# Per-example matrices made inside the loop, and the output put in order by ScalarE and VectorE, in a four-layer conditional residual kernel

## What is computed

```python
x = x + _L0_cond_ref(x, cond_128, ...)             # mixing
x = x + _L1_cond_ref(x, cond_128, ..., fside_S_0)  # convolution
x = x + _L2_cond_ref(x, cond_128, ...)             # mixing, other weights
x = x + _L3_cond_ref(x, cond_128, ..., fside_S_0)  # convolution, other weights

# mixing (L0, L2), K = 8
h = gelu(embedding @ W0 + b0); h = gelu(h @ W1 + b1)
att = softmax(h @ W2 + b2)
agg_w = einsum('bk,koi->boi', att, weight[..., 0]);  agg_b = att @ bias_k
out = einsum('boi,bih->boh', agg_w, x) + agg_b[:, :, None]

# convolution (L1, L3), 9 taps, 4 groups of 32 channels
out = conv(x, weight, padding=4, feature_group_count=4)
out = out + einsum('nd,od->no', c, c_weight)[:, :, None] + bias[None, :, None]
```

## Time and profile before

| | us |
|---|---|
| median of 3 runs | 2982.37 (2981.94 to 2983.42) |
| the profiled execution, its own time | 2982.91 |
| its span in the trace, first to last instruction | 2981.1 |
| TensorE matmuls, busy | 2905.9 (97%) |
| TensorE weight loads, busy | 2885.6 (97%) |
| VectorE, busy | 1312.3 (44%) |
| ScalarE, busy | 1552.4 (52%) |
| GpSimd, busy | 1551.1 (52%) |
| chain of work that ended last: share on TensorE | 97% |
| all DMA | 493.88 MB, 60.9% of 16 engines' span |
| TensorE's granted clock, mean | 0.985 |

### The profile page before, as it was taken

How to read it: one execution, slowest core, us unless ns; L and a number is a source line. 1 busy time by engine, 2 the same in 40 slices (tenths; PEclk the granted TensorE clock), 3 DMA queues, 4 the chain that set the end, 5 groups by cost and what they waited for, 6 DMA issues and landing times.

```text
span 2981.1 us, 121239 instructions
## 1 busy us (share of the span) xinstructions
PE 2905.9 (97%) x49252; PEld 2885.6 (97%) x49252; DVE 1312.3 (44%) x2142; ACT 1552.4 (52%) x2358; POOL 1551.1 (52%) x1796
## 2 busy tenths in 40 slices
PE   4899999999999999999999999999999999999997
PEld 2799999999999999999999999999999999999996
DVE  5344444444444444444444444444444444444441
ACT  4455555555555555555555555555555555555552
POOL 0455555555555555555555555555555555555552
PEclk7899999999999999999999999999999999999998
DMA  7465665665665665665665655655655656656653
GB/s 312 106 178 157 163 173 157 165 171 158 165 170 158 166 169 158 167 168 158 171 164 158 173 162 158 175 160 158 178 157 159 179 156 161 178 155 162 176 156 110
DMA packets 339978, 493.88 MB, mean 166 GB/s; under 512 B 59624, under 2 KB 190832, under 8 KB 322288
## 3 DMA queue, kind: packets, MB, share of 16 engines
q1 hardware_dynamic: 339952, 493.51, 60.9%
HBM read 208.06 MB, written 150.99 MB: 120 GB/s over the span
## 4 chain that ended last, share of the span: by engine, by line
PE 97%; DMA 1%; DVE 1%; ACT 0%; SPq 0%; issue 0%; POOL 0%; POOLq 0%; DVEq 0%; ACTq 0%
PE ps L317 72%; PE ps L302 24%; DMA mixed<-work 1%; DMA conv_raw<-conv_w 0%; SPq L228 0%; DVE work L558 0%; ACT work L412 0%; DVE y L542 0%; DVE y L587 0%; PE ps L279 0%; DMA work<-mix_b 0%; ACT xp L399 0%; PE ps L251 0%; POOL work L642 0%; DMA m_raw<-mixed 0%
## 5 line engine op out<-in xcount | busy, mean ns | idle before, releaser
L317 PE MATMUL ps<-y,conv_parts 32*128 32x512 f32 x36864 | 2667.9, 390 | 3.2 <-DVE y L587 3.2
L317 PEld LDWEIGHTS ps<-y,conv_parts 32*128 32x128 f32 x36864 | 2547.7, 184 | 9.1 <-DVE y L587 4.1
L587 DVE SCALAR_TENSOR_TENSOR y<-ps,bias,y 128x512 fp32r<-128x512 f32 x1536 | 1085.3, 750 | 1446.9 <-ACT y L438 1440.2
L438 ACT ACTIVATE y<-ps,bias 128x512 fp32r<-128x512 f32 x1536 | 1046.4, 690 | 683.8 <-PE ps L317 646.3
L635 POOL TENSOR_TENSOR xp<-x_t,xp 128x512 fp32r<-128x512 f32 x512 | 647.0, 1300 | 0.0
L302 PE MATMUL ps<-xp,m_parts 32*128 32x512 f32 x6144 | 621.1, 391 | 24.2 <-POOL xp L635 24.2
L628 POOL TENSOR_TENSOR m_parts<-m_raw,m_parts 128x512 fp32r<-128x512 f32 x256 | 331.7, 1296 | 585.5 <-ACT m_parts L444 585.4
L302 PE MATMUL ps<-y,m_parts 32*128 32x512 f32 x6144 | 618.9, 390 | 0.1
L302 PEld LDWEIGHTS ps<-xp,m_parts 32*128 32x128 f32 x6144 | 560.7, 184 | 25.9 <-issue 24.4
L302 PEld LDWEIGHTS ps<-y,m_parts 32*128 32x128 f32 x6144 | 562.2, 183 | 0.7 <-issue 0.5
L624 POOL COPY bias<-bias_table 128x4 f32 (+1 forms) x512 | 102.0, 200 | 816.5 <-DMA work<-work 662.5
(11 more groups left out here) (38 smaller groups left out, 37.3 us busy)
## 6 DMA issues: line engine op xcount, KB each, us to landing
x_t<-x SPq DMA_DIRECT2D x512, 256.0 KB, 5.1
work<-work SPq DMA_DIRECT2D x2048, 64.0 KB, 2.0
out<-work SPq DMA_DIRECT2D x128, 1024.0 KB, 4.8
m_raw<-mixed SPq DMA_DIRECT2D x1024, 64.0 KB, 4.4
mixed<-work SPq DMA_DIRECT2D x8, 2048.0 KB, 7.9
work<-mix_w SPq DMA_DIRECT2D x2, 2048.0 KB, 12.7
conv_raw<-conv_w SPq DMA_DIRECT2D x2, 768.0 KB, 10.8
work<-small SPq DMA_DIRECT2D x1, 852.0 KB
```

The lines of the kernel that those rows point to most:

```text
L317: ins = nc.tensor.matmul(ps[:, 4 + t, :], conv_parts[layer][rows, w, s, :], src[rows, a, p_in, q:q + N], start=(k == 0), stop=(k == CONV - 1))
L438: nc.scalar.activation(dst, src, ACT.Identity, bias=bias[layer][:, k:k + 1]).then_inc(high_set[layer], 1)
L587: nc.vector.scalar_tensor_tensor(out=dst, in0=src, scalar=bias[layer][:, k:k + 1], in1=high.bitcast(fp32), op0=ALU.add, op1=ALU.subtract). ...
```

## The change

Matrices are no longer made ahead. The attention of all examples is spread over all partitions by 16 fp32 matmuls against the identity and kept in `att_table`, with a ninth entry of 1. The eight weight matrices, with the identity as a ninth, lie in `mix_sb` as 128x(128x9). For each example and layer one multiplication (`prod`, 1152 elements per partition) and one sum over the innermost nine (`m_sum`) give the matrix; SP stores it in DRAM (64 KB) and loads it back in the old four-piece form. The multiplication of layer 0 is on VectorE, that of layer 2 on GpSimd (`scale`), both sums on VectorE. The 16 moves and `in_time` are replaced by 16 copies of 32 partitions x 512 from `o_ph` to `o_t`, phases 0 and 1 on ScalarE, 2 and 3 on VectorE. The last example goes from PSUM straight into `x_t` in eight pieces on each side and out in four stores. The loads are put in another order, x is split before the network is done, the second convolution's weights are prepared in step 0, the Gelu table is loaded ahead, the context matmuls come after the attention, and a convolution takes its 12 shifts by input phase first. Biases of layers 0 and 2 are one column in place of four.

The core of the diff:

```diff
+        MOVES = (("act", "act", "dve", "dve"),) * G
+
+        def moves(e):
+
+            return [(g, p) for g in range(G) for p in range(PH) if MOVES[g][p] == e]
+
+        def block(g, p):
+
+            return (o_t[CG * g:CG * (g + 1), :].rearrange("c (n p) -> c p n", p=PH)[:, p, :],
+                    o_ph[CG * p:CG * (p + 1), g, :])
...
+            def store_matrix(layer, j):
+
+                sp.wait_ge(summed[layer], j + 1)
+                sp.dma_start(scratch[layer // 2][bass.ds(j, 1)].rearrange("s c o -> (s c) o"), m_sum[layer][:]).then_inc(stored[layer], 16)
+
+            def load_matrix(layer, j, first):
+
+                if not first and layer == 0:
+                    sp.wait_ge(m_set[layer], j)
+                sp.wait_ge(stored[layer], 16 * (j + 1))
+                if not first and layer == 2:
+                    sp.wait_ge(m_set[layer], j)
+                for q in range(G):
+                    sp.dma_start(m_raw[layer][CG * q:CG * (q + 1)],
+                                 scratch[layer // 2][bass.ds(j, 1)].rearrange("s (g c) o -> (s c) g o", g=G)).then_inc(m_in[layer], 16)
+
+            sp.dma_start(room[:, 0:FIRST], small[:, 0:FIRST]).then_inc(first_in, 16)
...
             def step(i, inner):
+                if has(i, inner, -1):
+                    load_matrix(0, i + 1, not inner and i == -1)
                 if has(i, inner, 0):
-                    if inner or i >= 1:
-                        sp.wait_ge(m_set[2], i)
-                    load_matrix(2, i)
-                if has(i, inner, 2):
-                    for g in range(G):
-                        sp.wait_ge(phases_set, nth(i - 2, g))
-                        for p in range(PH):
-                            sp.dma_start(o_ch[CG * g:CG * (g + 1), p, :], o_ph[CG * p:CG * (p + 1), g, :]).then_inc(shuffled[p], 16)
+                    load_matrix(2, i, not inner and i == 0)
+                if has(i, inner, -2):
+                    store_matrix(0, i + 2)
+                if has(i, inner, -1):
+                    store_matrix(2, i + 1)
                 if has(i, inner, -2):
                     sp.wait_ge(x_low_set, 4 * (i + 2))
                     load_x(i + 2)
-                    sp.wait_ge(m_set[0], i + 2)
-                    load_matrix(0, i + 2)
-                if has(i, inner, 2):
-                    sp.wait_ge(in_time_set, 4 * (i - 1))
-                    sp.dma_start(out[i - 2], o_t).then_inc(out_done, 16)
+                if has(i, inner, 2) and (inner or not is_last(i)):
+                    sp.wait_ge(moved, G * PH * (i - 1))
+                    sp.dma_start(out[i - 2], o_t[:]).then_inc(out_done, 16)
+                if not inner and is_last(i):
+                    for g in range(G):
+                        sp.wait_ge(out_act, 2 * (g + 1))
+                        sp.wait_ge(out_dve, 2 * (g + 1))
+                        sp.dma_start(out[i - 2][CG * g:CG * (g + 1)],
+                                     flat(x_t, "g n")[CG * g:CG * (g + 1)]).then_inc(out_done, 16)
 
             steps(step)
             with sp.Fori(3, B - 2) as i:
                 step(i, True)
             last_steps(step)
-            sp.wait_ge(out_done, 16 * B)
-
-        @block.tensor
+            sp.wait_ge(out_done, 16 * (B - 1 + G))
...
+                nc.tensor.matmul(ps[:, 4 + l, 0:K], hidden1[:, l, :], w2_sb[:, l, :], start=True, stop=True).then_inc(logit_mm, 1)
+            for l in range(2):
+                pe.wait_ge(att_set, l + 1)
+                for k in range(K):
+                    last = nc.tensor.matmul(ps[:, 6 - 2 * l + k // 4, k % 4 * B:(k % 4 + 1) * B],
+                                            att_sb[:, l, k:k + 1].broadcast_to([128, 128]), ident, start=True, stop=True)
+                    if k % 4 == 3:
+                        last.then_inc(att_mm, 1)
+            for l in range(2):
...
+                if before and (inner or not is_last(i)):
+                    if inner or i > 2:
+                        act.wait_ge(out_done, 16 * (i - 2))
+                    act.wait_ge(phases_set, 4 * (i - 1))
+                    for g, p in moves("act"):
+                        nc.scalar.copy(*block(g, p)).then_inc(moved, 1)
...
+            def att_rows(l):
+
+                dve.wait_ge(att_mm, 2 * l + 2)
+                nc.vector.tensor_copy(att_table[:, :, l, 4:K].rearrange("c j k -> c k j"),
+                                      ps[:, 7 - 2 * l, :].rearrange("c (k j) -> c k j", k=4)).then_inc(table_dve, 1)
+
+            def matrix(layer, j, first):
+
+                l = layer // 2
+                if layer == 0:
+                    if first:
+                        dve.wait_ge(mix_in[layer], 16)
+                        dve.wait_ge(ones_set, 1)
+                        dve.wait_ge(table_act, l + 1)
+                        dve.wait_ge(table_dve, l + 1)
+                    else:
+                        dve.wait_ge(summed[layer], j)
+                    nc.vector.tensor_tensor(prod[layer][:], mix_sb[layer][:],
+                                            att_table[:, bass.ds(j, 1), l, :].broadcast_to([128, C, K + 1]),
+                                            ALU.mult).then_inc(scaled[layer], 1)
+                dve.wait_ge(scaled[layer], j + 1)
+                if not first:
+                    dve.wait_ge(stored[layer], 16 * j)
+                nc.vector.tensor_reduce(m_sum[layer][:], prod[layer][:], AX_X, ALU.add).then_inc(summed[layer], 1)
+
...
                 if now:
                     for q in range(G):
                         low(0, i, q, segment(LOW, q), by_phase(q), segment(HIGH, q))
+                if now and has(i, inner, -1):
+                    x_high(i + 1, False)
+                if has(i, inner, -2):
+                    matrix(0, i + 2, False)
                 if has(i, inner, -1):
-                    x_high(i + 1, not inner and i == -1)
+                    matrix(2, i + 1, not inner and i == -1)
...
                 if last:
                     for p in range(PH):
                         low(2, i - 1, p, y3[:, LOW, p, 1:N + 1], ps[:, p, :], y3[:, HIGH, p, 1:N + 1])
+                if has(i, inner, 2) and (inner or not is_last(i)):
+                    if inner or i > 2:
+                        dve.wait_ge(out_done, 16 * (i - 2))
+                    dve.wait_ge(phases_set, 4 * (i - 1))
+                    for g, p in moves("dve"):
+                        nc.vector.tensor_copy(*block(g, p)).then_inc(moved, 1)
...
+            def scale(j, first):
+
+                if first:
+                    pool.wait_ge(mix_in[2], 16)
+                    pool.wait_ge(ones_set, 1)
+                    pool.wait_ge(table_act, 2)
+                    pool.wait_ge(table_dve, 2)
+                else:
+                    pool.wait_ge(summed[2], j)
+                nc.gpsimd.tensor_tensor(prod[2][:], mix_sb[2][:],
+                                        att_table[:, bass.ds(j, 1), 1, :].broadcast_to([128, C, K + 1]),
+                                        ALU.mult).then_inc(scaled[2], 1)
+
...
                     x_low(i + 1)
+                if now and has(i, inner, -1):
+                    scale(i + 1, False)
                 if before and (inner or i - 1 < B):
                     pool.wait_ge(phases_set, 4 * (i - 1))
                     set_bias(3, i - 1)
                 if now:
                     matrix_low(2, i)
-                if before:
-                    if inner or i > 2:
-                        pool.wait_ge(out_done, 16 * (i - 2))
-                    for p in range(PH):
-                        pool.wait_ge(shuffled[p], 16 * G * (i - 1))
                 if last and (inner or i < B):
                     pool.wait_ge(low_set[2], 4 * i)
                     set_bias(2, i)
-                if before:
-                    in_time(i - 2)
-
```

480 lines of the change are left out of this document (212 added, 268 removed).

## The result

The change makes the kernel slower: 3479.01 us median (3477.63 to 3479.83, four runs) against 2982.15, a ratio of 1.1665, 95% interval [1.1644, 1.1685]. The profiled execution spans 3477.6 us, 496.5 more than the 2981.1 of before. The forecast was 3303 us, range 3000 to 3560: the direction and the kind of cause were right, the size was 176 us short.

A forecast was written before the change was run, and what follows sets the result against it. TensorE bounds the kernel at 22.30 us per step; a new VectorE-GpSimd loop makes it 25.4. 2981.1 - 59 - 14 + 3 = 2911, plus 126 x 3.1 = 391, plus 1.3: 3303 us, range 3000 to 3560.

The forecast's parts named there:

- It can only lose inside the steps: In the 126 repeating steps: TensorE's matmuls stay the same in number and size, so no step under 22.30 us.
- V: Loop VectorE, GpSimd, VectorE, closed by the second sum waiting for `scale`: 25.4 us per step, 3.1 over TensorE's; 57%.
- the 8 that were named as a sign: In the profile after: VectorE's longest wait, on GpSimd's `scale` before the second sum, some 8 us per step.
- the copy: VectorE's 32-partition copy of 512 with a 16-byte destination step: 0.45 us each, 3.6 for eight, from 0.34 to 0.59.
- S: Loop through TensorE, ScalarE and VectorE, with ScalarE's eight copies: 21.6 to 24.4 us, under 25.4, so hidden.
- copies over 1.2 us: A sign that the forecast is wrong: a step floor set by ScalarE's copies, at over 1.2 us each.
- Rival 4: TensorE pauses before each convolution 3 and its clock drops: step at least 25.65 us, about 3335, up to 3450; 14%.
- Rival 1: No multiply hold-off, early `matrix_low` and 0.34 us copies close the loop at 22.3 us, TensorE the bound: 2912 us; 15%.
- Rival 2: Copies don't overlap and pay the full stride: 0.68 us each, 27.2 us per step, 3530 us; 8%.
- Start-up: Before the first loop matmul: it comes at 26.6 us instead of 85.75, 59 us less, range 52 to 63.
- Opening steps: The two steps before the steady stretch: GpSimd's added subtraction and `scale` ahead of the second matrix give back 3 us.
- Closing: After the last `o_ph` starts: direct PSUM writes and 256 KB stores take 6 to 7 us instead of 20.7, 14 less.

The follow-up runs named there:

- contiguous: The whole change, but each of the sixteen copies writes its 512 elements side by side instead of every fourth; 3208.88 us, ratio 1.0758.
- copies_alone: The kernel before the change with only the output half: 16 copies in place of the DMA moves and GpSimd copies, matrices made ahead; 3483.88 us, ratio 1.1678.
- no_dve_copies: The whole change without VectorE's eight copies, so phases 2 and 3 of the output are not written; 3441.61 us, ratio 1.1537.
- sum_last: The whole change with VectorE's sum of matrix 2 behind `low(2)` and the copies, and its store behind the output's; 3434.02 us, ratio 1.1513.
- best: Matrix half alone against the kernel before, SP's old order plus two stores, matrix 2's sum at VectorE's step end, `x_high(0)` behind the network; 3073.44 us, ratio 1.0305.
- sum_last_no_act: The whole change with VectorE's sum of matrix 2 at the end of its step and ScalarE's eight copies left out; 3147.38 us, ratio 1.0552.
- out_later: Matrix half alone, matrix 2's sum last; output stored a step later, twelve moves before the x and matrix 0 loads, four behind, `scale` before `x_low`; 3069.92 us.

## Why the prediction came out as it did

- **"It can only lose inside the steps".** Right. TensorE needs the same 22.3 us, and gained nothing there in any run.
- **V's sum, 25.4.** Confirmed as a mechanism: 26.1 alone, VectorE waiting for `scale` ahead of the second sum. Term by term: `scale` 2.54 (2.8), sum 1.27 (1.3), `low(2)` 2.75 (2.85), `low(1)` and `low(0)` 5.74 (5.68). The multiply and GpSimd did hold each other off, once each: `x_low` took 6.38 and not 5.05, 1.33 more, about the multiply's own 1.35, and the multiply 2.45, 1.10 more. But `matrix_low` had started ahead of it, so from `x_high` to the end of `x_low` are 8.53 us, where 9.1 were forecast. VectorE's wait in front of the second sum is 4.82 us, and not the 8 that were named as a sign, since its own operations ahead of it took longer. The mis-sized term is the copy: 0.64, not 0.45, 1.5 us per step. 0.64 is outside the 0.34 to 0.59 that I drew from 128-element rows.
- **"ScalarE has a loop of its own ... under 25.4, so hidden".** This is the step that failed. With its terms corrected S is 26.6: copies of 1.13 and not 0.7 to 1.05 (9.1 us in place of at most 8.4), and a convolution 3 that takes 9.9 us in place of 8.4. The copy was taken as 0.49 and 0.2 to 0.55 for the stepped destination; no row shows the 0.49, and contiguous has 0.64 and 0.49. Against the 26.1 of V alone neither is enough by itself: with the copies as measured and no slower clock the sum is 11.2 + 2.8 + 0.6 + 9.1 + 1.4 = 25.1, and with the slower clock and copies of 1.05 it is 11.2 + 1.5 + 2.8 + 0.6 + 8.4 + 1.4 = 25.9. The three runs in which S stands alone (copies_alone, no_dve_copies, sum_last) have 26.3. I gave copies over 1.2 us as the point from which S decides; that point left out the clock.
- **Rival 4, the clock.** Its mechanism came about: 3.41 us at 1.2 GHz in 101 of 126 steps. The argument against it was wrong: other row groups were to end their mixing in the pause, but TensorE ran no matmul for 2.67 us. I set it beside V, where convolution 3 is no term of the loop. It belongs to S. A rival should be added to each loop that runs through the engine, not to the likeliest one alone.
- **Rival 1, the loop closes under 22.30.** Of its three conditions one came about: `matrix_low` starts 0.75 us after `x_high`, 6.4 on the forecast's clock. The hold-off and the copies went the other way.
- **Rival 2, copies at full stride cost.** Its 0.68 is close to VectorE's 0.64; whether each copy waited for the one before, as it says, was not tested. The Trainium skill's figure in "Vector Engine (DVE) Microarchitecture Reference", section 5.2, cited there, gave an estimate of 0.71, nearer the measurement than my 0.45; the measured one decides.
- **Start-up, 26.6 against 34.8.** `x_high(0)` was counted as free within the network. It stands ahead of the logits on VectorE and x landed at 11.29, so the spreading matmuls start at 17.27, where 12 was forecast; in best, where `x_high(0)` is moved, they start at 9.17. The first layer's eight then took 3.6 us in place of 3.3 (the row's 5.98 are those of both layers), and VectorE's copy behind them 1.12 in place of 0.7. A second delay lies behind: in after the cast of matrix 0 ends at 30.94, but GpSimd has `scale(0)` (2.49) to do first and starts `matrix_low` at 33.45. In best the first loop matmul therefore comes at 34.17 in spite of the 8 us: its `matrix_low` starts at 32.81, behind `x_low(0)`, the layer biases, the identities and `scale(0)`. The forecast of this stretch followed VectorE's queue and not GpSimd's.
- **Opening steps, 3 forecast, 12.8 measured.** Between the same two marks TensorE idled 9.90 us, and 1.67 before: two pauses of 4.19 and 4.05 us came new, both for a `low` of VectorE's that stood behind the second sum, which had waited 9.50 and 7.24 us for `scale`. So V holds the opening steps too. The other 4.6 us are busy time, 50.80 us in place of 46.22, at a granted clock of 0.77 over the stretch in place of 0.87. The forecast priced GpSimd's added work there, not these waits.
- **Closing, -14 forecast, -12.2 measured.** The two numbers agree by luck. From the last convolution's first finished bank to the end are 13.3 us, in place of 20.7 before, so 7.4 less and not 14: each engine makes eight direct writes of 1.15 us, where two were counted, and ScalarE's come behind its eight copies of the example before, from 3456.30 to 3465.26, a queue that the forecast did not name. The other 4.8 us lie ahead of that, between the last two outputs (13.1 us in place of 17.9), where TensorE's granted clock was 1.00 after and 0.81 before.

The 176 us that were missed: 156 in the steps, 8 in the start-up, 10 in the opening steps, 2 at the end. That the time stayed within the range owes something to chance: V and S have almost the same length. Had ScalarE's copies cost 1.4 us, S would have been about 28.7 and the range left. So would V with copies of about 0.85, such as VectorE had in sum_last_no_act (an estimate: 26.1 + 8 x 0.21 = 27.8).

## What to carry to other kernels

When TensorE is full and the others are half busy, add up every closed loop through the step, not the engines' totals; when the likeliest loop is found, price the second one with the same care, with each slow-down (a stepped destination, a lower clock after a pause) in each loop that contains it. A DMA issue has a place in its queue like any instruction: a store that waits for something made in the same step delays all that stands behind it. And work that was done once ahead of a loop is cheap: moving it into the steps gained 51 us once, and every order of it that ran cost about 1.2 us or more in each of 126 steps.

## What the runs showed of the hardware

- A copy of 32 partitions by 512 fp32 costs 0.64 us on ScalarE and 0.45 on VectorE when it writes side by side, and 1.13 and 0.64 with a destination step of 16 bytes. On VectorE four 128-partition casts of the same length take 1.43 us, 0.36 each: a copy on a quarter of the partitions is not cheaper than that.
- The hold-off between VectorE and GpSimd goes both ways: four casts took 2.53 to 3.62 us for 1.43, the multiply 2.45 for 1.35, GpSimd's `x_low` 6.38 for 5.05. Single copies of 32 partitions are held off as well: 1.36 and 1.63 us for 0.64 in sum_last_no_act.
- TensorE's granted clock fell to the lower level for 3.4 us after the engine had stood at convolution 3 for 2.6 to 3.5 us, in 101 of 126 steps of after; in the other 25 it had stood for 2.6 to 2.7 us and the clock did not fall. In sum_last_no_act, where it stood there for 1.5 us, the mean clock was 0.994, against 0.944 in after. In contiguous it stood for 1.2 to 2.0 us in 82 steps, and the clock fell in 42.
- A 64 KB move within SBUF landed 2.0 us after its issue in the median of before, and 3.8 us after it in out_later, issued right behind the loads of x and of matrix 0.
